# q, k, v and first feed-forward matmuls as three float32r products of high and low parts, with their steps rearranged

## What is computed

```python
h = _layernorm(x, axis=-1) * (1 + ca) + sa
q = split_heads(lora_linear(h, wq, aq, bq))          # k and v in the same way
scores = jnp.einsum('bhqd,bhkd->bhqk', q, k) / jnp.sqrt(jnp.float32(HEAD_DIM))
attn = softmax(where(causal, scores, -inf))
ctx = jnp.einsum('bhqk,bhkd->bhqd', attn, v)
x = x + ga * lora_linear(ctx, wo, ao, bo)
h = _layernorm(x, axis=-1) * (1 + cb) + sb
logits = jnp.einsum('bsd,ed->bse', h, Wg) + bg       # the two best of four, w their softmax scores
base = jnp.einsum('bsd,fd->bsf', h, Wi)
lora = jnp.einsum('bser,efr->bsef', jnp.einsum('bsd,erd->bser', h, A), B)
x = x + gb * einsum('bse,bsed->bsd', w, relu(base[:, :, None, :] + lora) @ Wo.T)
```

## Time and profile before

| | |
|---|---|
| median of 3 runs | 1978.09 us (1977.63 to 1978.61) |
| the profiled execution | 1980.25 us, its span 1978.5 us |
| PE busy | 1802.2 us, 91% of the span |
| DVE, ACT, POOL busy | 1234.0, 941.8, 532.9 us |
| prologue | 0 to 100 us |
| body of batch 0 | 100 to 279 us |
| bodies of batches 1 to 6 | 279 to 1652 us, 229 us each (the last 226) |
| body of batch 7 | 1652 to 1862 us |
| epilogue | 1862 to 1978.5 us |

### The profile page before, as it was taken

The page is one execution under the profiler, slowest core; times in us unless marked ns, Lnnn a source line. Parts: engine busy times, 40 slices in busy tenths (PEclk is TensorE's granted clock), DMA queues, the critical chain, the costliest instruction groups (busy, mean ns, idle before and its releaser), DMA issues.

```text
span 1978.5 us, 31549 instructions
## 1 busy us (share of the span) xinstructions
PE 1802.2 (91%) x10868; PEld 942.1 (48%) x10868; DVE 1234.0 (62%) x2681; ACT 941.8 (48%) x1701; POOL 532.9 (27%) x833
## 2 busy tenths in 40 slices
PE   7698889999989999999989999899999999899868
PEld 5343344454544555454644545444554545344535
DVE  3676577657676567756686577766677555753131
ACT  2255465544555455544455445544455444544320
POOL 2112122322313222233223222133222232133223
PEclk9789899999999999999999999999999999899979
DMA  7613432313321313223323223213222222220000
GB/s 179 146 54 91 82 82 55 76 42 75 74 80 39 94 44 81 68 41 76 85 60 71 52 67 85 67 41 92 60 47 66 45 76 57 39 42 23 25 0 22
DMA packets 249862, 128.69 MB, mean 65 GB/s; under 512 B 158214, under 2 KB 244834, under 8 KB 249708
## 3 DMA queue, kind: packets, MB, share of 16 engines
q1 hardware_dynamic: 245564, 125.61, 26.4%
q10 hardware_dynamic: 4144, 1.07, 0.4%
HBM read 83.06 MB, written 41.97 MB: 63 GB/s over the span
## 4 chain that ended last, share of the span: by engine, by line
PE 71%; DVE 17%; ACT 5%; issue 3%; SPq 2%; DMA 2%; POOL 0%; POOLq 0%; DVEq 0%; ACTq 0%
PE dense L855 11%; PE ov L911 11%; PE st L896 10%; PE mxs L880 8%; PE dense L998 6%; PE dense L936 5%; PE dense L841 5%; PE dense L849 4%; DVE negm L1311 4%; DVE negm_left L1311 3%; PE dense L861 3%; PE mxs L884 2%; PE dense L928 2%; ACT probs L1046 2%; SPq L651 2%
## 5 line engine op out<-in xcount | busy, mean ns | idle before, releaser
L1046 ACT ACTIVATE probs<-st 128x512 f32<-128x512 f32 (+1 forms) x1216 | 672.6, 576 | 717.6 <-PE st L896 715.1
L1311 DVE TENSOR_REDUCE negm<-mxs 128x1 f32<-128x384 f32 (+4 forms) x736 | 444.9, 617 | 258.0 <-PE mxs L884 255.3
L896 PE MATMUL st<-q_st,k_st 98*128 98x512 bf16 (+3 forms) x1536 | 451.8, 332 | 24.8 <-ACT probs L1046 17.4
L880 PE MATMUL mxs<-k_st,q_st 96*128 96x512 bf16 (+3 forms) x1280 | 401.3, 324 | 34.9 <-DVE negm_left L1311 20.8
L1311 DVE TENSOR_REDUCE negm_left<-mxs 128x1 f32<-128x512 f32 x512 | 343.1, 687 | 141.7 <-PE mxs L880 140.6
L911 PE MATMUL ov<-probs,v_g 128*32 128x512 f32 (+3 forms) x3072 | 332.0, 505 | 1.4 <-POOL probs L743 1.4
L855 PE MATMUL dense<-c_t,wi_t 128*128 128x512 f32 x512 | 266.3, 606 | 12.3 <-DVE second L1365 11.6
L880 PEld LDWEIGHTS mxs<-k_st,q_st 96*128 96x128 bf16 x1280 | 123.4, 98 | 269.9 <-issue 103.4
L756 POOL TENSOR_TENSOR hid<-hid,second 128x512 f32<-128x512 f32 x128 | 161.8, 1266 | 305.3 <-DVE second L1365 305.3
L896 PEld LDWEIGHTS st<-q_st,k_st 98*128 98x128 bf16 x1536 | 142.4, 99 | 169.6 <-ACT probs L1046 71.0
L740 POOL TENSOR_TENSOR fence<-fence 128x1 f32<-128x1 f32 x256 | 51.5, 201 | 621.8 <-ACT probs L1046 621.8
(11 more groups left out here) (165 smaller groups left out, 1700.8 us busy)
## 6 DMA issues: line engine op xcount, KB each, us to landing
q_st<-q_parts_scratch SPq DMA_DIRECT2D x384, 64.0 KB
k_st<-k_parts_scratch SPq DMA_DIRECT2D x384, 64.0 KB
q_parts_scratch<-q_part SPq DMA_DIRECT2D x16, 768.0 KB, 3.3
k_parts_scratch<-k_part SPq DMA_DIRECT2D x16, 768.0 KB, 5.2
xin<-in_L_attn_x SPq DMA_DIRECT2D x8, 1024.0 KB, 5.8
values_scratch<-v_rows SPq DMA_DIRECT2D x32, 256.0 KB, 2.1
v_g<-values_scratch SPq DMA_DIRECT2D x128, 64.0 KB, 3.9
x<-in_L_attn_x SPq DMA_DIRECT2D x16, 512.0 KB, 4.3
```

The source lines that it names most:

```text
L880: last = nc.tensor.matmul(mxs[:, bank_m, j * n:j * n + left], q_st[0:KS, slot, h0 + j, qt * P:(qt + 1) * P], k_st[0:KS, slot, h0 + j, k0:k ...
L896: last = nc.tensor.matmul(st[:, score_bank(ch, kt, h0), j * n:(j + 1) * n], k_st[0:KS + 2, slot, h0 + j, kt * P:(kt + 1) * P], q_st[0:KS + ...
L1046: nc.scalar.activation(probs[:, par, h0:h0 + heads, 0:n], st[:, score_bank(ch, kt, h0), 0:heads * n].rearrange("p (j q) -> p j q", q=n), A ...
L1311: nc.vector.tensor_reduce(dst[:, h0:h0 + heads], src, axis=AX.X, op=ALU.max, negate=True).then_inc(max_free, 1)
```

## The change

The q, k and v projections and the first feed-forward matmul no longer run as float32 products. Each operand is held as a high part, rounded to the type float32r, and a low part, the remainder in float32r; the product is the sum of three float32r products, high by high, high by low and low by high. What changes with it:

- **PE.** `project` and `hidden` issue three products of 512 columns for each 128 features, `value_rows` (v) three of 256. Output projection, routing, the second feed-forward matmul and the transposes stay as they are.
- **The parts.** Weights are split in the setup: ACT writes the high part, DVE subtracts (`SPLIT_SETUP`, 7 setup steps). For `h_t` DVE copies the high part (`hs`, two steps of two 128x512 copies) and POOL subtracts (`hl`, four of 128x512), per batch. For `c_t` POOL does both: `ch` (four copies of 128x512) and `cs` (four subtractions). The four pieces 3 to 6 of `ln2`, eight tiles of 128x256, go from DVE to POOL.
- **Memory.** The low parts lie in the place of `h_t` and `c_t`, and the high part of `h_t` in the place of `xin`, so `xin` is loaded for the next batch only after the last projection: step `xin` goes from unit 3 to unit 31, behind `rs` on the SP queue, and `ls1` starts in unit 35 instead of 39. `q_part` and `k_part` hold one half of the heads (`ot`) instead of two, so a `pj` on ACT waits until all `ps` before it have landed. v's staging lies in `second` and `hid`; ACT waits for its transfers once, at `fx` of tile 4.
- **Places.** In a body no q or k tile stands before unit 21 (there were five). The v tiles go from units 7, 8, 12, 13 to 10, 15, 19, 20. `t2` goes to unit 12, `rt` and `rx` to 13, the six pieces of `ro` to one a unit, 14 to 19, and the feed-forward tiles start in unit 24 behind four q and k tiles and end in unit 46. `ps` goes to 25 and 38, `xl` of the first half to 37. In the prologue the setup steps 9 to 18 stand before the maxima of the first group, and the second four q and k tiles among them. The body of batch 0 has its first four q and k tiles in units 8 to 14 and its second four in 27 to 30.

```diff
     slots = {u: [] for u in range(GROUPS * NU)}
     chains = {u: [] for u in range(GROUPS * NU)}
+    begins = {u: [] for u in range(GROUPS * NU)}
...
     if post:
         slots[1] += [("ct", i) for i in range(4)]
         for i in range(4):
             slots[2 + i] += opened("oa", i)
-            chains[4 + i].append(("ls2", i))
-        for i, u in enumerate((7, 8, 8, 8, 9, 9, 9)):
+            chains[5 + i].append(("ls2", i))
+        for i, u in enumerate((9, 9, 9, 10, 10, 11, 11)):
             chains[u].append(("ln2", i))
-        slots[10] += [("t2", i) for i in range(4)]
-        slots[11] += [("rt",), ("rx",)]
-        for i, u in enumerate((12, 12, 13, 13, 14, 14)):
+        slots[12] += [("t2", i) for i in range(4)]
+        if pre:
+            for half in range(2):
+                chains[half].append(("hs", half))
+            for i in range(4):
+                begins[3 + i].append(("hl", i))
+        for i in range(4):
+            begins[14 + i].append(("ch", i))
+            begins[16 + i].append(("cs", i))
+        slots[13] += [("rt",), ("rx",)]
+        for i, u in enumerate((14, 15, 16, 17, 18, 19)):
             chains[u].append(("ro", i))
-        slots[16] += [("mt", v) for v in range(2)] + [("rb", half) for half in range(2)]
+        for i, p in enumerate((("mt", 0), ("mt", 1), ("rb", 0), ("rb", 1))):
+            slots[21 + i * pre].append(p)
...
         for i, q in enumerate(dense):
-            slots[17 + 30 * i // len(dense)] += q
+            slots[21 + 26 * i // len(dense)] += q
...
         extra[PS_UNITS[0]] = ("ps", 0, 0)
         extra[PS_UNITS[1]] = ("ps", 1, 0)
-    if ahead and post:
-        extra[3] = ("xin",)
     if ahead:
+        extra[31] = ("xin",)
...
         plan.append(("xl", 1))
-    extra[34] = ("xl", 0)
+    extra[37] = ("xl", 0)
...
+        plan += begins[u]
...
-POOL_IDLE = frozenset("mx pv qk nm ce ov vg ms rs t1 t2 ls1 ls2 ln1 ln2 ro ct rt rx".split())
+POOL_IDLE = frozenset("mx pv qk nm ce ov vg ms rs t1 t2 ls1 ls2 ln1 ro ct rt rx hs".split())
 LATE_MAXIMA = 9
 SHORT_STEPS = 10
-PJ_UNITS = (0, 6, 10, 11, 15)
-PJ_SLOTS = (5, 9, 13)
-V_UNITS = (7, 8, 12, 13)
-PS_UNITS = (17, 36)
+PJ_UNITS = ()
+PJ_SLOTS = (0, 1, 2, 3, 9, 10, 11, 12)
+V_UNITS = (10, 15, 19, 20)
+PS_UNITS = (25, 38)
...
     plan += values[2] + values[3] + [("rs", g, half, g) for g in range(2) for half in range(2)] + [("vg", 0)]
-    plan += pj[1][:6] + [("su", N_PROJECTION_SETUP)]
-    beside = [pj[1][6:]] + [[("su", i)] for i in range(N_PROJECTION_SETUP + 1, N_SETUP)]
+    plan += [("su", i) for i in range(N_PROJECTION_SETUP, N_SETUP)]
     mx = [("mx", 0, *s) for s in max_steps()]
-    for i, s in enumerate(beside):
-        plan += s + mx[4 * i:4 * i + 4]
-    assert 4 * len(beside) >= len(mx)
+    tiles = len(pj[1]) // 2
+    for i in range(tiles):
+        plan += mx[len(mx) * i // tiles:len(mx) * (i + 1) // tiles] + pj[1][2 * i:2 * i + 2]
     plan += [("ms",), ("ps", 1, 0), ("nm", 0)] + score_steps(0, *UNITS[0])
     return plan
...
-        w_t = sb("w_t", [P, 4, KC, D])
-        wi_t = sb("wi_t", [P, KC, F])
+        w_hi = sb("w_hi", [P, 3, KC, D], F32R)
+        w_out = sb("w_out", [P, KC, D])
+        w_lo = sb("w_lo", [P, 3, KC, D], F32R)
+        wi_t = sb("wi_t", [P, KC, F], F32R)
+        wi_lo = sb("wi_lo", [P, KC, F], F32R)
...
-        xin = sb("xin", [P, T, D])
+        xin, xin_r = shared("xin", [P, T, D], "xin_r", [P, T * D])
         x1 = sb("x1", [P, T, D])
-        h_t = sb("h_t", [P, KC, S])
+        h_t, h_lo = shared("h_t", [P, KC, S], "h_lo", [P, KC, S])
...
-        c_t = sb("c_t", [P, KC, S])
-        v_rows = sb("v_rows", [P, 2, 2, D])
+        c_t, c_lo = shared("c_t", [P, KC, S], "c_lo", [P, KC, S])
+        c_hi = sb("c_hi", [P, KC, S], F32R)
         v_g = sb("v_g", [P, 2, T, HG, 32])
-        q_part = sb("q_part", [P, 2, 3, S], BF16)
-        k_part = sb("k_part", [P, 2, 3, S], BF16)
+        q_part = sb("q_part", [P, 3, S], BF16)
+        k_part = sb("k_part", [P, 3, S], BF16)
...
+                elif kind == "hl":
+                    half, k = divmod(a[0], 2)
+                    cols = slice(half * HB, (half + 1) * HB)
+                    pool.wait_ge(h_high, of_half(KC * done("hs"), half))
+                    nc.gpsimd.tensor_tensor(h_lo[:, k, cols], h_t[:, k, cols], h_hi[it >= 0][:, half, k, :].bitcast(F32),
+                                            ALU.subtract).then_inc(h_split, 1)
+                elif kind == "ln2" and a[0] >= 3:
+                    pool.wait_ge(norm_chain, (done("normed") + 1) * NORM_LINKS)
+                    for t in range(2 * a[0] - 6, 2 * a[0] - 4):
+                        last = nc.gpsimd.tensor_scalar(x2n[:, t, :], x1[:, t, :], nt[:, 1, t:t + 1],
+                                                       nt[:, 3, t:t + 1], ALU.mult, ALU.add)
+                    last.then_inc(norm2_ready, 1)
...
+                elif kind in ("ch", "cs"):
+                    half, k = divmod(a[0], 2)
+                    cols = slice(half * HB, (half + 1) * HB)
+                    if kind == "ch":
+                        for i in range(2):
+                            after(pool, dense_free[i], done(f"t2 bank{i}"))
+                        nc.gpsimd.tensor_copy(c_hi[:, k, cols], c_t[:, k, cols]).then_inc(c_high, 1)
+                    else:
+                        pool.wait_ge(dense_full, done("rt full"))
+                        pool.wait_ge(c_high, done("cs") + 1)
+                        nc.gpsimd.tensor_tensor(c_lo[:, k, cols], c_t[:, k, cols], c_hi[:, k, cols].bitcast(F32),
+                                                ALU.subtract).then_inc(c_split, 1)
                 elif kind == "fb":
                     half, ft = a
...
-
-            def token_rows(db, n, kind, i):
-
-                src, m = (h_t, 2) if kind == "vp" else (c_t, 3)
+            def project(db, k, which, ot, half, it):
+
+                high, low = h_hi[it >= 0][:, half, k, :], h_lo[:, k, half * HB:(half + 1) * HB]
+                m, cols = WNAMES.index(which), slice(ot * P, (ot + 1) * P)
+                for i, (w, h) in enumerate(((w_hi, high), (w_hi, low), (w_lo, high))):
+                    last = nc.tensor.matmul(db[:, :], w[:, m, k, cols], h, start=(k == 0 and i == 0),
+                                            stop=(k == KC - 1 and i == 2))
...
+            def value_rows(db, n, i, it):
+
                 t = 2 * i + n
                 for k in range(KC):
-                    last = nc.tensor.matmul(db[:, n * D:(n + 1) * D], src[:, k, t * P:(t + 1) * P],
-                                            w_t[:, m, k, :], start=(k == 0), stop=(k == KC - 1))
+                    high = h_hi[it >= 0][:, t // 4, k, t % 4 * P:(t % 4 + 1) * P]
+                    low = h_lo[:, k, t * P:(t + 1) * P]
+                    for j, (h, w) in enumerate(((high, w_hi), (high, w_lo), (low, w_hi))):
+                        last = nc.tensor.matmul(db[:, n * D:(n + 1) * D], h, w[:, 2, k, :],
...
             def hidden(db, k, half, ft):
 
-                nc.tensor.matmul(db[:, :], wi_t[:, k, ft * P:(ft + 1) * P], c_t[:, k, half * HB:(half + 1) * HB],
-                                 start=(k == 0), stop=False)
+                rows, cols = slice(ft * P, (ft + 1) * P), slice(half * HB, (half + 1) * HB)
+                for i, (w, c) in enumerate(((wi_t, c_hi), (wi_t, c_lo), (wi_lo, c_hi))):
+                    nc.tensor.matmul(db[:, :], w[:, k, rows], c[:, k, cols], start=(k == 0 and i == 0), stop=False)
...
                     which, ot, half = a
-                    dst = (q_part if which == "q" else k_part)[:, ot, :, half * HB:(half + 1) * HB]
-                    if isinstance(it, int) and it < 0:
-                        act.wait_ge(gates_out, 16)
-                        act.wait_ge(blank_out, 16)
-                    after(act, parts_out[ot], done(f"ps{ot}") * (2 * 16))
+                    dst = (q_part if which == "q" else k_part)[:, :, half * HB:(half + 1) * HB]
+                    for i in range(2):
+                        after(act, parts_out[i], done(f"ps{i}") * (2 * 16))
                     nc.scalar.copy(dst[:, 0, :], db[:, :]).then_inc(part1_ready, 1)
                 elif kind == "vp":
...
+                elif kind == "hs":
+                    half = a[0]
+                    for i in range(2):
+                        after(dve, dense_free[i], done(f"t1 bank{i}"))
+                    for k in range(KC):
+                        nc.vector.tensor_copy(h_hi[it >= 0][:, half, k, :], h_t[:, k, half * HB:(half + 1) * HB]
```

152 lines of the change are left out of this document (104 added, 48 removed).

## The result

The changed kernel takes 2027.6 us (median of 4 runs, 2022.3 to 2030.3) where the kernel before took 1977.9 beside it: a ratio of 1.025, 95% interval 1.0236 to 1.0264. It is slower by 50 us; forecast was 62 us faster, so the sign was wrong, and the time lies far above the range.

The account below looks back on a forecast made before the run. PE, busy for 91% of the span, was taken as the bound. Middle bodies -51, batch 0 -4, batch 7 -5, epilogue -5 and prologue +3 gave -62 from 1980.25 us profiled: 1918.3, or 1916 us as median, range 1895 to 1945 (0.70).

Parts of the forecast that it names:

- A body's idle time and clock: Middle bodies: idle time grows by 3.2 us, against 11.7 us less PE work, giving 220.5 us; clock stays 1.00.
- the second rival: Light stretches: PE waits in units 6 to 9 and 14 to 18, clock falls; up to 6.6 us a body, 1956; chance 0.10.
- the sign that I had named: Units 14 to 18: a falling clock there would show the forecast wrong; no size given for the sign.
- The largest term, 4.0 for the light units: Middle body: nine units losing all dense work last 3.12 us for 2.65 of PE work, 4.0 us more idle.
- The loads: Middle body, `rs` loads around units 7 and 0: shrunken units cover less of the 9.5 us, 1.7 us more idle.
- Hidden in sum: POOL's added subtractions, copies and norm tiles, some 130 us on 533, hidden; nothing counted, up to 2 us a body in range.
- Costs less than its bunch: Middle body: routing chain at one piece a unit beside reductions, formerly visible as 1.71 us in unit 15, saves 1.5 us idle.
- The prologue: Prologue: projections -2.5, copy and subtractions +3.2, moved q and k tiles +4, setup 0, other projections -1.7: +3 us.
- The products: PE: float32r at 0.216 us per 512 columns saves 0.42 us a tile, 11.7 a middle body, 93.7 in all.
- the mask of unit 11: POOL, unit 11: norm tiles of 2 to 4 us stand ahead; asked a unit ahead, covering about 2.5 us; nothing counted.
- Half rate: PE rival: float32r takes 0.43 us per 512 columns, 193 us more, about 2165 us; chance 0.05.
- loads in series: PE rival: each float32r product waits for its weight load, 74 us more, 2052; chance 0.03.

Follow-up runs that it names:

- the places alone: The kernel before, with float32 products and no splits, given the changed kernel's places in the bodies of batches 1 to 7: 2009.9 us, ratio 1.0164.
- the order of before: The changed kernel with three of the last four q and k tiles under the first loads again, setup steps among the maxima: 2019.8 us, ratio 1.0221.
- the nine other kernels above: Follow-up kernels that share the changed kernel's epilogue; the text does not list which nine; their epilogue takes 113.4 to 117.6 us.
- three arrangements: Changed kernel with spread q and k tiles, later subtractions and the prior prologue order, 1978.1 us; two versions with places altered to mend waits, 1982.4 and 1982.9 us.
- the feed-forward alone: The mended-places kernel with float32r only in the first feed-forward matmul, q, k and v plain float32, second-half c_t work in units 30 and 31: 1954.5 us, ratio 0.9875.

## Why the prediction was wrong

Of the sum's steps, in the order of their damage:

- **A body's idle time and clock: the step that failed.** Forecast was 4.0 - 1.5 - 1.0 + 1.7 = +3.2 us idle, and no term for the clock. Measured: +6.8 us idle and 6.6 us of clock a body. The mechanism of the second rival (PE waits in light stretches, the clock falls) was right, and its size of up to 6.6 us a body too; I gave it 0.10 because the middle bodies stood at 1.00 before, where no wait of PE in batch 4 was longer than 1.3 us. The change makes three of 2.0 to 2.6, and the sign that I had named, a clock that falls in units 14 to 18, came true in unit 16. By units the idle time is (us a body, mean of batches 1 to 5; the places alone are the kernel of the second experiment):

  | units | forecast | before | places alone | changed |
  |---|---|---|---|---|
  | 0, 6, 7, 8, 11, 14, 16, 17, 18 (light) | +4.0 | 2.0 | 2.0 | 4.3 |
  | 9, 13 (loads) | +1.7 | 0.9 | 4.0 | 4.6 |
  | 10, 12, 15 | -1.5 | 4.0 | 0.1 | 0.8 |
  | 21 | none | 0.0 | 1.8 | 2.0 |
  | 22 to 47 | -1.0 | 5.5 | 6.4 | 7.1 |
  | 1 to 5, 19, 20 | none | 0.5 | 0.6 | 0.8 |

  The largest term, 4.0 for the light units, was wrong: with the places alone they are no more idle than before, and of the 4.3 us now 2.6 are the one wait in unit 16. The loads cost twice what I had for them, and no term held unit 21, where PE waits for DVE's maxima (0.9 us in batch 4) and for ACT (1.0).
- **POOL's work: a step that I took for free.** "Hidden in sum" is true, POOL is at 33%, but DVE's routing chain pays: the subtractions moved behind it give 5.0 us a body back, as much as the 4.8 that separate the places alone from places and splits. "Costs less than its bunch", -1.5 us for the spread routing, holds with the places alone (1.9 us idle in units 14 and 15 before, 0.1 then, 0.4 in unit 16 in both) and not with subtractions beside it, which cost 2.6 in unit 16.
- **The prologue**, +3 forecast, +23 measured. 5.6 us is the norm behind DVE's splits, which I had put under the loads at 0; 4.6 the casts and subtractions (forecast 3.2), and 9.3 came back with the order of before; I had 4 for it. The other 3.6 no run takes apart. By the account of above, PE's work fell by 3.7 us, idle time grew by 14.1 and the clock's share by 12.7 (9.1 to 21.8; 0.77 instead of 0.88), nearly all of it behind the first v tile.
- **The products**, -11.7 a body forecast, -7.4 measured: -8.5 against the same places with float32 products (0.232 instead of 0.216 us is 2.3 of the 3.2 missing), and 1.1 us more busy time that the places alone show too; the more frequent waits, behind which a product's record is longer, are the likely reason, not a shown one.
- Batch 0 (-4 forecast, -2.2) has the smaller product gain (PE's work -3.7 for -5.0), batch 7 (-5, -2.7) that (-4.9 for -6.7) and 2.6 us more idle for 1.7. In the epilogue (-5, -3.5) the work fell by 4.5, idle time grew by 4.4 for 1.7, and 3.4 us less at half clock are luck: in the nine other kernels above with the same epilogue it takes 113.4 to 117.6 us, in six of them over 117, where the kernel before has 116.8 and the changed one 113.4. `xin`, ACT's waits for stores and the mask of unit 11 behaved as forecast.

From 1916 us: six bodies of 4.3 (products), 3.6 (idle) and 6.6 (clock) too little are 87 us, the prologue 20, the rest 6: 2029, where 2027.6 was measured. Half rate and loads in series did not occur: the load of a float32r product takes 190 ns, under the product ahead of it. The v tiles had their 0.41 us although their loads are recorded with 189 ns too: these records stand 0.12 us apart and overlap each other, so the 31 us that the range held for loads of that length did not come.

What stays open: why the idle time of a body keeps to 17 us through three arrangements. Each wait names a queue order on DVE or POOL, but I have no account of which order is the bound.

## What to carry to other kernels

Price a change that makes the bound engine's work cheaper by what the helpers must do for it, and not by their busy shares: 28 subtractions on an engine busy for 27% cost 30 us, because they stood beside a chain of DVE instructions with two operands in SBUF. When work is taken out of a unit, look at what it covered; a new wait of 2.0 to 2.5 us in a dense stream cost 3.7 to 4.2 us where 3.4 us at half clock came with it. And try such a change part by part: the splits of `c_t` serve 16 tiles of 512 columns a body and stand on no path of the prologue, and the feed-forward alone was worth more than the whole.

## What the runs showed of the hardware

- In a row of float32r matmuls one of 512 columns starts 0.232 us before the next, at half clock 0.427, one of 256 columns 0.117; the weight load is recorded with 190 ns like a float32 one and shows nowhere in these distances.
- With PE's waits of 1.8 to 2.9 us in units 9, 13 and 16 the granted clock stood at 0.50 for 3.4 or 6.8 us in 17 of 18 cases (batches 1 to 6 of the changed kernel); matmuls added into 12 of these waits kept it at 1.00 there, and a kernel with more work was faster.
- A subtraction of 1.27 us on POOL held DVE instructions of 0.19 us with two operands in SBUF for up to 1.2 us, and left those with one as they were (0.19). It goes the other way too: a POOL instruction of one column, 0.19 us, took 0.62 beside a DVE copy of 1024 columns (the kernel before with added subtractions, unit 14 of batch 4).
